# A recurrence and a routed feed-forward block on one core: up products three tiles ahead, routing and weight splits spread over more tiles, tile scales on another engine, row transfers in pairs

## The reference, cut to what matters

```python
# cond: x is (128, 128, 256) after reshaping in the kernel's order; 2 sequences of 1024 steps
xp = einsum('ntd,dh->nth', x, Wx) + b
def step(prev_h, xp_t):
    next_h = tanh(xp_t + prev_h @ Wh)
    return next_h, next_h
_, h = scan(step, h0, swapaxes(xp, 0, 1))
# ffn on the 2048 states h
shared = silu(h @ shared_w1.T) @ shared_w2.T          # 256 -> 1024 -> 256
top_k_gates, top_k_idx = top_k(h @ gate_w.T, 2)       # 8 experts, the best two
gates = softmax(top_k_gates)
selected = sum over the two experts: gate * (silu(h @ w1[e].T) @ w2[e].T)
return x + shared + selected
```

## Time and profile before

| | us |
|---|---|
| median of 3 executions | 384.38 |
| lowest, highest | 378.96, 389.39 |
| profiled execution, its own time | 382.84 |
| its span in the trace | 381.0 |
| PE busy in the span | 355.0 (93%) |
| DVE, ACT, POOL busy | 197.2, 239.0, 106.4 |

### The profile page before, as it was taken

One profiled execution on the slowest core, in us unless ns is written; L12 is line 12 of the kernel. 1 busy time (PEld: TensorE's weight loads), 2 busy tenths in 40 slices (PEclk: granted clock), 3 DMA queues, 4 the chain that ended last, 5 costly groups with the idle time before them and its releaser, 6 DMA issues.

```text
span 381.0 us, 8845 instructions
## 1 busy us (share of the span) xinstructions
PE 355.0 (93%) x2440; PEld 251.4 (66%) x2441; DVE 197.2 (52%) x421; ACT 239.0 (63%) x462; POOL 106.4 (28%) x99
## 2 busy tenths in 40 slices
PE   7979999988998787999999999999999999999971
PEld 6758899945664554566666666666666666666660
DVE  0599999978999953863323332233333233332310
ACT  3878888975965764665555566556666555666510
POOL 0100100000038888600114333322233322333331
PEclk9999999999999999999999999999999999999996
DMA  7999999518799996999998898878888888998981
GB/s 225 430 430 433 421 400 335 153 27 141 132 207 228 246 279 180 228 187 226 174 140 146 158 165 150 157 143 150 148 165 147 157 140 151 151 162 146 158 106 15
DMA packets 167325, 75.60 MB, mean 198 GB/s; under 512 B 149504, under 2 KB 163968, under 8 KB 166016
## 3 DMA queue, kind: packets, MB, share of 16 engines
q1 hardware_dynamic: 155408, 61.93, 66.1%
q0 software_dynamic: 6864, 9.11, 16.3%
q10 hardware_dynamic: 5024, 4.20, 4.5%
HBM read 23.68 MB, written 16.53 MB: 106 GB/s over the span
## 4 chain that ended last, share of the span: by engine, by line
PE 73%; DVE 8%; SPq 6%; DMA 5%; issue 3%; ACT 2%; POOL 1%; ACTq 0%; POOLq 0%
PE py L1170 32%; PE z L1062 30%; PE z L1078 4%; DVE w_slots L581 3%; SPq L352 3%; PE z L1011 2%; DMA space<-recurrence_w 2%; SPq L378 2%; PE z L1043 2%; DVE w_slots L580 2%; DMA space<-space 2%; DMA space<-x_cols 1%; PE py L1011 1%; PE z L1024 1%; ACT space L912 1%
## 5 line engine op out<-in xcount | busy, mean ns | idle before, releaser
L1170 PE MATMUL py<-w_slots,space 128*128 (+1 forms) x1272 | 150.5, 274 | 10.8 <-DMA space<-recurrence_w 5.3
L1170 PEld LDWEIGHTS py<-w_slots,space 128*128 128x128 f16 x1272 | 124.2, 98 | 40.2 <-issue 11.2
L1062 PE MATMUL z<-w_slots,x 128*128 (+1 forms) x636 | 145.9, 379 | 2.1 <-issue 2.1
L1062 PEld LDWEIGHTS z<-w_slots,x 128*128 128x128 f16 x636 | 62.0, 98 | 66.9 <-issue 3.5
L912 ACT ACTIVATE space<-z,tile_scales 128x512 f32<-128x512 f32 x106 | 71.8, 677 | 49.7 <-PE z L1062 37.0
L488 POOL DMA_INDIRECT out<-space x37 | 58.7, 1586 | 154.7 <-ACT space L936 65.1
L637 DVE SCALAR_TENSOR_TENSOR recurrence_w<-space,tile_scales,recurrence_w 128x512 f16<-128x512 f32 x54 | 40.3, 751 | 74.1 <-ACT recurrence_w L919 60.2
L637 DVE SCALAR_TENSOR_TENSOR space<-space,tile_scales 128x512 f16<-128x512 f32 x52 | 38.7, 752 | 61.5 <-ACT space L919 55.2
L581 DVE SCALAR_TENSOR_TENSOR w_slots<-w_slots,w_scale 128x1024 f16<-128x1024 f32 x36 | 46.2, 1283 | 1.0
L919 ACT ACTIVATE recurrence_w<-space,tile_scales 128x512 f16<-128x512 f32 x54 | 39.0, 722 | 8.7 <-ACT space L912 3.0
L919 ACT ACTIVATE space<-space,tile_scales 128x512 f16<-128x512 f32 x52 | 37.5, 722 | 7.8 <-ACT space L912 2.7
(11 more groups left out here) (121 smaller groups left out, 161.5 us busy)
## 6 DMA issues: line engine op xcount, KB each, us to landing
w_slots<-weights SPq DMA_DIRECT2D x8, 2048.0 KB, 31.6
sorted_rows<-pad_row SPq DMA_DIRECT2D x1, 5070.0 KB, 59.0
w_slots<-weights SPq DMA_DIRECT2D x2, 1024.0 KB, 9.6
space<-x_rows ACTq DMA_DIRECT2D x16, 128.0 KB
out<-space ACTq DMA_DIRECT2D x16, 128.0 KB
space<-x_cols SPq DMA_DIRECT2D x3, 512.0 KB, 9.0
space<-recurrence_w SPq DMA_TRANSPOSE x55, 2.4
space<-space SPq DMA_TRANSPOSE x52
```

Source lines behind the costliest of these rows:

```text
L1062: last = nc.tensor.matmul(Z[u % 2][h][:], x16[:, u, x_part, k], weight(f, k * HID + h * BANK, BANK, part), start=k == 0 and x_part == 0 an ...
L1170: last = nc.tensor.matmul(PY[p][:, 0:D], hiddenT[:, p, low, q], weight(f, MATRIX + q * D, D, part), start=q == 0 and not low and part == 0 ...
```

## The change

PE runs `up` of the shared tiles three tiles ahead instead of two (`LEAD`): `up(2)` and then `up(g + 3)` before `down(g)`. With two pairs of accumulators, `up` now waits half by half for the silu of the tile two back. The sorted tiles keep their distance of two, so `down(13)` follows `down(12)` directly. ACT makes the first silu before it learns whether the speculation held, so the buffer `hidden` moves, and the branch for a failed speculation is rewritten (it is not taken with these inputs; PE jumps over two blocks instead of one).

DVE's routing steps come one shared tile later or between halves, `shared_y` runs three tiles behind, the splits follow a new table, and `route_tiles` moves from tile 4 to tile 10. The products of scales go to POOL, behind the scatters, as twelve instructions that each wait for the one before (`make_scales`); ACT, DVE and PE wait for `tiles_ok` before the first sorted tile. POOL's last `reduce_bounds` moves behind the first two scatters. The ring of row tiles has six buffers, and rows go out in another order. x and the outputs move in pairs of tiles (256 KB each), the first two loads of x issued early by SP.

```diff
-SORT_RING = 8
+SORT_RING = 6
+LEAD = 3
-ROWS_AT = {0: (0, 1, 2), 1: (3,), 3: (4, 5), 4: (6, 7), 5: (8, 9), **{t - 4: (t,) for t in range(10, TILES)}}
-STATES_AT = {0: (2, 3), 1: (4, 5), **{t - 4: (t,) for t in range(6, TILES)}}
+ROWS_AT = {1: (2,), 2: (3, 4), 3: (5,), 4: (6,), 5: (7, 8), 6: (9, 10), 7: (11,), 8: (12, 13), 9: (14,), 10: (15,)}
+STATES_AT = {0: (2, 3), 1: (4,), 2: (5, 6), **{t - 4: (t,) for t in range(7, TILES)}}
-SPLITS_AT = {3: (22, 23), 5: (24,), 6: (25, 26), 7: (27,), 8: (28, 29), 9: (30,), 10: (31,), 11: (32, 33), 12: (34,), 13: (35,)}
-HIGHS_FROM = 6
+SPLITS_AT = {4: (22,), 5: (23,), 6: (24,), 7: (25, 26), 8: (27, 28), 9: (29, 30), 10: (31,), 11: (32, 33), 12: (34,), 13: (35,)}
+HIGHS_FROM = 7
...
@@ SP
-            for g in range(TILES):
+            turn_first()
+            turn_row(0)
+            turn_part(0, 0, 0)
+            turn_row(1)
+            turn_part(0, 0, 1)
+            for g in range(1, TILES):
                 turn(g, g % 2)
                 for t in ROWS_AT.get(g, ()):
                     turn_row(t)
...
@@ POOL
+            def make_scales():
...
+                for n in range(3):
+                    step(nc.gpsimd.tensor_mul(scale_parts, is_expert,
+                                              ffn_scales[:, n, 1:FFNS].unsqueeze(1).broadcast_to([P, SLOT_TILES, E])))
+                    for half in (E // 2, E // 4):
+                        step(nc.gpsimd.tensor_add(scale_parts[:, :, 0:half], scale_parts[:, :, 0:half], scale_parts[:, :, half:2 * half]))
+                    step(nc.gpsimd.tensor_add(tile_scales[:, TILES:ALL_TILES, n], scale_parts[:, :, 0], scale_parts[:, :, 1]))
+                pool.sem_inc(tiles_ok, 1)
...
+                v = t - SORT_RING // 2
+                if 0 <= v < TILES - SORT_RING:
+                    waited(sorted_ok[v % SORT_RING], 16 * TOP * (v // SORT_RING + 1))
+                    nc.gpsimd.tensor_copy(hr[:, v % SORT_RING, D:ROW], meta[:, v + SORT_RING]).then_inc(row_copied, 1)
...
+            make_scales()
@@ DVE
+            for g in range(2, TILES):
+                n = 16 * (g // 2)
                 hidden_low(g, g % 2, n, 0)
                 hidden_low(g, g % 2, n, 1)
+                if g >= LEAD:
+                    shared_y(g - LEAD)
...
-                if g >= AHEAD:
-                    shared_y(g - AHEAD)
@@ PE
                 for h in range(HALVES):
+                    if arrived is None:
+                        pe.wait_ge(hidden_ok, g * HALVES - (2 * HALVES - h - 1))
+                    elif h == 0:
+                        pe.wait_ge(hidden_ok, (g - 1) * HALVES)
                     up_half(u, f, h, up_mm)
...
+            up(AHEAD, AHEAD, SHARED)
             for g in range(TILES):
+                if g + LEAD < TILES:
+                    up(g + LEAD, (g + LEAD) % RING, SHARED)
```

More of the change, by code:

```diff
@@ L277, in build @@
         meta_in, idx_ok, idx_step = sem("meta_in"), sem("idx_ok"), sem("idx_step")
-        stored = [sem(f"stored{u}") for u in range(RING)]
+        stored = [sem(f"stored{v}") for v in range(2)]
         added = [sem(f"added{u}") for u in range(RING)]
@@ L460, in _ @@
             for t in range(TILES):
+                u = t % SORT_RING
                 if t >= SORT_RING:
@@ L496, in _ @@
             pool.wait_ge(padded_out, 16)
-            for u in range(RING):
-                pool.wait_ge(stored[u], 16 * TILES // RING)
+            for v in range(2):
+                pool.wait_ge(stored[v], 16 * PAIRS // 2)
             for t in range(COMMON_TILES):
@@ L750, in route_tiles @@
                                              iota_e[:].unsqueeze(1).broadcast_to([P, SLOT_TILES, E]), ALU.is_equal))
-            def route_scales():
-                for n in range(3):
-                    link(nc.vector.tensor_mul(scale_parts, is_expert,
-                                              ffn_scales[:, n, 1:FFNS].unsqueeze(1).broadcast_to([P, SLOT_TILES, E])))
-                    last = nc.vector.tensor_reduce(tile_scales[:, TILES:ALL_TILES, n], scale_parts, AX.X, ALU.add)
-                    if n < 2:
-                        link(last)
-                last.then_inc(tiles_ok, 1)
@@ L888, in _, with tile_scale, silu_first @@
             find_last(0)
+            def tile_scale(g, n):
+                return tile_scales[:, bass.ds(g, 1), n:n + 1].rearrange("p a n -> p (a n)")
+            def silu_first(done):
+                nc.scalar.activation(hidden[:, 0:BANK], Z[0][0][:], ACT.Silu, scale=tile_scale(0, 0)).then_inc(done, 1)
+            act.wait_ge(split_ok, 1)
+            act.wait_ge(up_mm, 1)
+            silu_first(hidden_ok)
             act.wait_ge(drift_known, 1)
@@ L936, in sorted_y @@
                 nc.scalar.mul(ys[:, u], PY[u % 2][:, 0:D], y_scale[:, bass.ds(t, 1)]).then_inc(y_ok, 1)
-            act.wait_ge(split_ok, 1)
             hidden_half(0, 0, None, 0)
-            for t in STATES_AT[0]:
-                shared_rows(t, x_hi_ok)
+            shared_rows(2, x_hi_ok)
             hidden_half(0, 0, None, 1)
-            for n in range(2):
-                nc.scalar.dma_start(x_res[:, n], x_tiles[n]).then_inc(x_res_in[n], 16)
+            shared_rows(3, x_hi_ok)
             act.wait_ge(gap_ok, 1)
@@ L964, in _ @@
                     nc.scalar.mul(high, whole, scale).then_inc(high_ok, 1)
-                if g > AHEAD:
-                    store(g - AHEAD - 1)
+                if g >= LEAD + 2 and g % 2:
+                    store((g - LEAD - 2) // 2)
+            act.wait_ge(tiles_ok, 1)
             def expert(t, u, n, outs, indexed):
@@ L1056, in router, with general_pair @@
                 return last
+            def general_pair(r, i, p, first=False):
+                if not first:
+                    for k in range(K):
+                        pe.wait_ge(h_ok_general[k], i * 2 + (r * L))
+                for m in range(K):
+                    inject(p, i, m)
+                for u in range(2):
+                    if u:
+                        for k in range(K):
+                            pe.wait_ge(h_ok_general[k], i * 2 + (r * L + 1))
+                    for k in range(K):
+                        for m in range(K):
+                            last = nc.tensor.matmul(Z[p][m][:, u * COLS:(u + 1) * COLS], wh_sb[:, k, m * P:(m + 1) * P],
+                                                    column(k, i * 2 + u), start=False, stop=k == K - 1, skip_group_check=True)
+                            if k == K - 1:
+                                last.then_inc(z_mm_general[m], 1)
             def up_half(u, f, h, done):
@@ L1124, in _ @@
                 pe.wait_ge(up_mm, 2 * HALVES)
+                pe.wait_ge(hidden_ok, 1)
                 with pe.Fori(0, GENERAL_ROUNDS) as r:
-                    inject_first()
                     pe.wait_ge(start_ok_general, r + 1)
-                    round_(z_mm_general, h_ok_general, r)
+                    for i in range(2):
+                        general_pair(r, i, i, first=i == 0)
+                    with pe.Fori(1, L // 4) as j:
+                        for p in range(2):
+                            general_pair(r, j * 2 + p, p)
+            with pe.If(same != EXPECTED_SAME):
                 for k in range(K):
```

164 lines of the change are left out of this document (87 added, 77 removed).

## The result

| us | before | after |
|---|---|---|
| median (lowest to highest, runs) | 382.56 (378.96 to 389.39, 4) | 389.63 (388.92 to 390.89, 4) |
| profiled execution, its span | 382.84, 381.0 | 390.89, 389.1 |
| first up product | 77.88 | 79.54 |
| first scatter, end of the last | 110.09, 162.36 | 107.36, 161.41 |
| load of the first sorted tile (SP) | 165.59 | 166.44 |

The changed kernel is slower: ratio 1.0187, 95% interval 1.0123 to 1.025, so whether by more than 2% is open. The forecast was 376.2 with a range to 382.5. Some executions of a kernel ran up to 4% longer than its others, most of them at a lower granted clock, and ratios leave those out, so a ratio is not always that of the two medians.

A forecast was written before the change was run, and what follows sets the result against it. PE's waits before the first sorted up product were taken as the bound. Sorted rows at 164.0, later than PE's 159.2, moved its start from 170.60, gaining 6.6 us: 382.84 - 6.6 = 376.2, range 370.5 to 382.5.

The forecast's parts named there:

- Scales on POOL: Twelve chained POOL instructions after the last scatter: about 6 us, `tiles_ok` at 162.4, hidden behind the load's 164.0.
- The fourth rival: POOL's scales end last: above 14.2 us the kernel is slower than now, up to 385.5 us; chance 0.06.
- The upper bound of 16.9 us: Most the twelve POOL instructions could take: longest copy 1.24 us plus 0.17 handing over, times twelve.
- within 2%: Outcome band for the whole kernel, less than 2% (7.7 us) from the time before; chance 0.47.
- Slots ready and first scatter: DVE's slots at 103.5, with 2.1 us added work and one for row tile 2; first scatter at 104.0.
- Scatters: POOL's scatters: 52.3 us, less 2.05 of row-tile waiting, plus 1.0 for a reduction and 1.2 for copies; end 156.4.
- Loading back: Last scatter to first sorted up product: 3.2 us until the load, then 4.4, so up(s0) at 164.0.
- PE's own arrival: PE, without stops, is done with the products ahead of the first sorted up product at 159.2.
- The second rival: Hidden-row transposes stay the limit in the shared tiles: PE arrives near 169, 381 us; chance 0.22.
- Pairs of x and output: Moving x and outputs two tiles at a time: same bytes, half the transfers, off PE's path, no effect.
- DVE slows the scatters (third rival): DVE's splits among POOL's scatters hold them up 3 us: up(s0) at 167, 379 us; chance 0.12.

The follow-up runs named there:

- kernel 1: Changed kernel with the products of scales back on DVE, right behind `route_tiles`: 382.16 us, ratio 1.0035 to the kernel before.
- kernel 15: kernel 1 run once more, unaltered, for comparison on one chip: 383.48 us, ratio 1.0065 to the kernel before.
- kernel 13: kernel 1 with row tiles later in SP's queue, x and outputs in single tiles, second sorted load behind tile 14's transposes: 378.81 us, ratio 0.9953.
- kernel 7: kernel 1 with each scatter writing only 16 bytes of token data per row, experts' output missing: 379.71 us, ratio 0.995.
- kernel 10: kernel 1 with the sort's row tiles copied instead of transposed, so the experts' output is wrong: 379.56 us, ratio 0.9843.
- kernel 11: kernel 1 with x and outputs moved one tile at a time (128 KB) again: 381.75 us, ratio 0.9972.
- kernel 12: kernel 1 with row tiles 8 to 15 later in SP's queue, and x and outputs one tile at a time: 382.03 us, ratio 0.9951.
- kernel 2: Changed kernel plus a one-element-per-partition addition on POOL before it waits for `routed`: 391.49 us, ratio 1.0287.
- kernel 3: Changed kernel plus the same small POOL addition among the scatters, behind those of row tile 8: 385.49 us, one run.
- kernel 4: Kernel before with only the products of scales moved to POOL behind its scatters: 391.39 us, ratio 1.0309.
- kernel 9: kernel 1 with later row tiles, and loads of second sorted tile and token data behind tile 14's transposes: 382.0 us, ratio 0.9874.

## Why the prediction was wrong, point by point

*Scales on POOL: this step failed.* It put `tiles_ok` 6 us behind the last scatter, at 162.4 and hidden; it came 14.8 us behind, at 176.18, and PE stood 7.58 us for it. The twelve instructions were sized well (7.24 us against 6: 0.79 for 312 elements, 0.91 for the pair, 0.26 for 39). What was missing is a piece that no number of instructions scales, the 7.54 us ahead of the first. A gap of this kind stood in the rows: the 128x128 select, from which the sum took 0.28 us, had 8.1 us of idle time ahead of it, put down to "issue", and was read for its duration alone. The fourth rival is what happened, by another mechanism than it named: 14.8 us, just over its break-even of 14.2. The upper bound of 16.9 us did hold the truth; the chance of 0.06 was too small for a kind of instruction that POOL had not run in this program. The time of this rival, up to 385.5, was passed by all the same: the last scatter ended 5.0 us later than summed, and the clock fell. Had the scales been hidden as forecast, the kernel would have been where kernels 1 and 15 are, in the middle of "within 2%".

*The clock.* The prediction had no term for it. A stop of 7.58 us brought a loss of 2.6 us behind it.

*Slots ready and first scatter.* Forecast 26.1 us behind the first up product, measured 27.8 (27.9 in kernel 13). The sum was also short by 0.3: 100.74 + 2.1 + 1 is 103.8, not 103.5. The wait for row tile 2, for which one microsecond was put in, took longer; ACT after:

```profile
97.31 0.42 ACT L904 ACTIVATE x<-states 128x256 f16<-128x256 f32 x1 [2.96 <-DMA space<-x]
```

*Scatters.* Forecast 52.4 us from first to last, measured 54.1 in both; the sum took off 2.05 us of waiting for the last row tile, and it stayed: 2.70 us in the changed kernel, 2.63 and 1.56 in kernel 13. From the first up product on, POOL started 4.4 us sooner than before and ended 2.6 sooner (after), at 3.4 us a tile for 3.3.

*Loading back.* Right in sum: 7.6 us forecast, 7.9 in kernel 13 (159.58 to 167.43), though in other parts. The load went out 4.5 us behind the last scatter for 3.2, since it waits for that scatter to land, 5.26 us from its issue, and up(s0) came 3.3 behind the load for 4.4. Kernel 13's chain of waits:

```profile
158.62 5.26 DMA sorted_rows<-space
```

Together the sort's chain was forecast at 86.1 us and takes 89.9 (kernel 13). Of the 6.6 us of gain expected from it, 2.9 were there.

*PE's own arrival.* This is the second step that failed, and with the sort's chain it is why nothing is gained even where POOL's loss is undone (kernels 1 and 15): the stops were to fall away by the sooner sort alone, and they stayed. The rest of the sum was right: without stops it gave 81.3 us from the first up product (159.2 - 77.88). With the 8.2 us of stops at down products in the changed kernel, and 1.3 for the slow product behind the longest of them (4.10 for 2.78), that makes 90.8 for 90.6 measured. Its group of down products ahead of up(s0):

```profile
L1233 PE MATMUL py<-w_slots,space 128*128 128x256 f16 x336 | 41.1, 278 | 8.2 <-DMA space<-recurrence_w 6.4 <-DMA space<-space 0.9 <-issue 0.4
```

The second rival said that the transposes stay the limit, with PE at 169 and 381 us; measured were 170.12 (1.66 us of it by a late start), and 382.16 for kernel 1. It named the right thing, transposes that land late, but not all of why. In the changed kernel they took a median of 3.3 us where it was 2.4 (page of the profile, transfers; two profiles of kernel 1 had 2.8 and 3.2), and single ones far more (chain of waits):

```profile
space<-recurrence_w SPq DMA_TRANSPOSE x55, 3.3
```

```profile
137.86 6.46 DMA space<-recurrence_w
```

Kernels 7 and 10 took some of the stops away: 9.7 and 8.3 us for the 13.0 and 11.2 of kernel 1. Neither the bytes of the sort nor the row transposes alone are the cause, and what holds the rest up stays open.

*Pairs of x and output: "nothing".* Nothing else is shown. With the pairs undone the stops were 10.4 us for 13.0 or 11.2 (kernel 11) and 8.6 for 9.9 (kernel 12), changes of the size by which two profiles of one kernel differ, and the times stood.

*DVE slows the scatters (third rival).* The scatters took 1.8 us longer, not 3, and a longer wait for a row tile is in it. Whether DVE's splits hold up POOL was not tried.

## What to carry to other kernels

Before a small operation moves to an engine, look whether that engine has run this kind in this program, and what kind it ran before: the price of the first one may be more than that of all the rest. Read the idle time of a row as well as its duration: a gap without a named releaser is a price too, and it may lie elsewhere after the change. Where two chains end within a few microseconds of each other, add up both from one common start; a gain on one is worth no more than the distance to the other. And a bound that decides the sign deserves the chance of what is unknown, not of what the nearest row makes likely.

## What the runs showed of the hardware

- POOL stood 7.1 to 8.5 us, with nothing in the trace, when it went from PARTITION_ALL_REDUCE to TENSOR_TENSOR (7.54, 7.11, 8.46, 8.01, 7.74), and 6.76 us the one time that it went back (kernel 2). Indirect transfers and COPY between them neither cost it nor undid it (kernel 3). The Trainium skill, GPSIMD Engine Reference, section 2.1 (Instruction dispatch), says that the first call of a freshly loaded kernel pays about 6 us with no visible instruction, 5.95 measured. The traces agree in kind and are 0.8 to 2.5 us above; that POOL loads anything in these gaps, no trace shows.
- After 7.6 us without work PE's granted clock was 0.50 (1.2 GHz) in the window from 175, and 1.00 again (2.4 GHz) in the window from 185: some 2.6 us lost. In kernel 4 the stop of 9.54 us was followed by an up product of 4.80 us for 2.75. The length of the stop does not decide alone: before down(14) a stop of 2.81 us in kernel 1 was followed by a product of 4.19 us, and stops of 2.87 and 2.89 us in kernels 9 and 10 by products of 2.78.
- Transposes from on-chip memory to on-chip memory landed in 2.4 us in the median before. Single ones took far longer in the chains of waits: 7.22 us (kernel 1) and 6.98 us (kernel 9), within a microsecond of 512 KB of plain transfers, but also 7.00 us in kernel 13, where an output and an x of a single tile each, 256 KB together, went out at that moment. No run shows what such a transfer waits for.
